# Decoder layer on one core: routed rows computed seven tiles early, their products no longer woven into the dense ones

## What is computed

```python
logits = xn @ router_w
topv, topi = jax.lax.top_k(jax.nn.softmax(logits, axis=-1), K)          # K = 2
...
for e in range(E):                                                      # E = 8
    out = out + comb[:, e:e + 1] * _swiglu(xn, gate_up_w[e], down_w[e]) # gate clipped to +-10
out = out + _swiglu(xn, shared_gate_up_w, shared_down_w)
x = _layernorm(x + out.reshape(b, s, d))
```

## Time and profile before

| what | value |
|---|---|
| median of 3 runs (lowest, highest) | 1808.25 us (1808.15, 1811.41) |
| the profiled execution itself | 1811.44 us |
| its span in the profile | 1809.7 us, mean granted TensorE clock 0.987 |
| PE busy | 1730.8 us, 96% of the span |
| DVE, ACT, POOL busy | 1485.6, 1105.6, 265.6 us |
| experts (PE's first to last matmul) | 1665.4 to 1801.6 us |

### The profile page before, as it was taken

How to read it: one execution, slowest core, us unless ns; L and a number is a source line. 1 busy time by engine, 2 the same in 40 slices (tenths; PEclk the granted TensorE clock), 3 DMA queues, 4 the chain that set the end, 5 groups by cost and what they waited for, 6 DMA issues and landing times.

```text
span 1809.7 us, 31511 instructions
## 1 busy us (share of the span) xinstructions
PE 1730.8 (96%) x9280; PEld 867.8 (48%) x9280; DVE 1485.6 (82%) x2398; ACT 1105.6 (61%) x1355; POOL 265.6 (15%) x344
## 2 busy tenths in 40 slices
PE   6977999999999999999999999999999999998896
PEld 4854444444444444444444444444444444444674
DVE  7868988888888888888878797979787888775777
ACT  4554666666666666666666666666666666665554
POOL 4746992000000000000000000000000000001443
PEclk8989999999999999999999999999999999999999
DMA  5001210000000000000000000000000000001000
GB/s 166 2 1 35 69 41 1 0 0 0 0 0 0 0 0 0 0 0 0 0 0 0 0 0 0 0 0 0 0 0 0 0 0 1 0 2 33 2 2 13
DMA packets 17753, 16.68 MB, mean 9 GB/s; under 512 B 6047, under 2 KB 15907, under 8 KB 17318
## 3 DMA queue, kind: packets, MB, share of 16 engines
q1 hardware_dynamic: 17446, 15.48, 2.8%
q0 software_dynamic: 256, 0.53, 0.1%
HBM read 13.95 MB, written 2.06 MB: 9 GB/s over the span
## 4 chain that ended last, share of the span: by engine, by line
PE 88%; DVE 6%; ACT 3%; issue 3%; POOL 0%; DVEq 0%; DMA 0%; SPq 0%; POOLq 0%; ACTq 0%
PE PS L1732 87%; ACT p_arena L931 1%; DVE mxs L1583 1%; DVE mxs L1319 1%; ACT p_arena L924 1%; DVE z_arena L1616 0%; DVE w_arena L1100 0%; DVE w_arena L1274 0%; ACT z_arena L767 0%; ACT p_arena L921 0%; DVE acc L1621 0%; POOL w_arena L587 0%; DVE m_arena L1280 0%; DVE z_arena L1607 0%; PE PS L1741 0%
## 5 line engine op out<-in xcount | busy, mean ns | idle before, releaser
L921 ACT ACTIVATE p_arena<-PS 128x1024 f16<-128x1024 f32 (+1 forms) x480 | 484.8, 1010 | 531.1 <-PE PS L1732 530.9
L1732 PE MATMUL PS<-a_arena,z_arena 128*128 (+1 forms) x2832 | 746.3, 380 | 4.4 <-DVE a_arena L1338 4.1
L1732 PE MATMUL PS<-p_arena,z_arena 128*128 128x512 f16 x2800 | 740.4, 379 | 1.4 <-ACT p_arena L931 0.3
L1319 DVE TENSOR_REDUCE mxs<-PS 128x512 f32 (+1 forms) x900 | 582.5, 668 | 91.0 <-PE PS L1732 87.7
L1351 DVE TENSOR_TENSOR p_arena<-p_arena 128x1024 f16<-128x1024 f32 (+1 forms) x480 | 574.8, 1198 | 98.0 <-ACT p_arena L924 90.8
L924 ACT ACTIVATE p_arena<-PS 128x1024 f32<-128x1024 f32 (+1 forms) x480 | 481.6, 1003 | 0.0
L1732 PEld LDWEIGHTS PS<-a_arena,z_arena 128*128 (+1 forms) x2832 | 274.8, 98 | 331.8 <-DVE a_arena L1338 4.4
L1732 PEld LDWEIGHTS PS<-p_arena,z_arena 128*128 128x128 f16 (+1 forms) x2800 | 269.2, 98 | 311.9 <-ACT p_arena L931 8.8
L1732 PE MATMUL PS<-z_arena,a_arena 128*128 (+3 forms) x1024 | 353.8, 361 | 10.5 <-DVE mxs L1319 8.2
L699 POOL IOTA a_arena<- 128x512 f16 x1 | 0.6, 558 | 1289.8 <-DVE acc L1362 1289.8
L1732 PEld LDWEIGHTS PS<-z_arena,a_arena 128*128 (+1 forms) x1024 | 97.8, 98 | 144.0 <-DVE mxs L1319 26.5
(11 more groups left out here) (324 smaller groups left out, 1014.8 us busy)
## 6 DMA issues: line engine op xcount, KB each, us to landing
w_arena<-in_L_ffn_gate_up_w SPq DMA_DIRECT2D x8, 512.0 KB, 3.6
p_arena<-in_ctx SPq DMA_DIRECT2D x2, 1600.0 KB, 9.0
w_arena<-in_L_ffn_down_w SPq DMA_DIRECT2D x8, 256.0 KB, 4.0
a_arena<-in_L_xattn_Wkv SPq DMA_DIRECT2D x1, 1024.0 KB, 5.8
xg_dram<-VO SPq DMA_DIRECT2D x1, 975.0 KB, 8.8
w_arena<-in_x SPq DMA_DIRECT2D x1, 512.0 KB, 4.3
a_arena<-in_L_xattn_Wo SPq DMA_DIRECT2D x1, 512.0 KB, 6.8
w_arena<-in_L_xattn_Wq SPq DMA_DIRECT2D x1, 512.0 KB
```

The costliest lines, as they stand in the source:

```text
L921: s.activation(Phi[:, r % 3, 0:w], ps, ACT.Exp, scale=1 / SSC).then_inc(hi_ready, 1)
L1319: v.tensor_reduce(mxs[:, i, bass.ds(kb, 1)], PS[:, 6 + par, 0:w], AX.X, ALU.max).then_inc(mx_read, 1)
L1732: return t.matmul(o, l, r, start=start, stop=stop)
```

## The change

- The woven form is gone: every unit writes its whole gate, then small work part 0, then its whole up product, then part 1.
- Seven slots instead of four stand between shared 0 and shared 1, and the other eight follow one behind each of the first eight dense units (experts 0 and 1) instead of two per expert up to expert 5. `COMB_END` is unit 30 instead of 43.
- The norm of the second half starts behind clip 0, two pieces in each of units 0 to 3; its transpose moves from unit 2 to 5, its router from 5 to 10, its exponential from 9 to 14. The end of the first half goes in ten pieces instead of five.
- In the last block the first half's transposes move from step 4 to 5, its router from 6 to 8, what follows by two steps each, and the transposes of its first slots from step 25 to behind the last step.

```diff
-AHEAD = 4
+AHEAD = 7
...
         for i in range(4):
             order.append(("dense", e, i))
-            if i % 2 == 0 and k < SLOTS:
+            if k < SLOTS:
                 order.append(("slots", k, 0))
...
         for t in ALL_TILES:
-            put(p + 3 + t // 2, t % 2, "shared", half, t)
-    put(2, 1, "turned", 1, 0)
-    put(5, 1, "routed", 1, 0)
+            put(p + 3 + t, 1, "shared", half, t)
+    put(5, 1, "turned", 1, 0)
+    put(10, 1, "routed", 1, 0)
```

ACT (`half_act(0, 0)` from step 6 to 7, `half_act(0, 1)` from step 9 to 11; in the units):

```diff
-                if u == 3:
+                if u == 6:
                     half_act(1, 0)
-                elif u == 9:
+                elif u == 14:
                     half_act(1, 1)
```

DVE, `half_in_block` (one shift of two steps from the routing on), `half_done` and `side_work`:

```diff
-                elif st == 5:
+                elif st == 6:
                     dve.wait_ge(ld_fv, N_FV)
                     dve.wait_ge(xfT_ps, 1)
                     turned(0, 6).then_inc(xfT_v, 1)
-                elif st == 7:
+                elif st == 9:
                     turned_low(0)
...
-                    for t in ALL_TILES:
+                if piece < 2:
+                    for t in (2 * piece, 2 * piece + 1):
                         last = v.tensor_tensor(acc[:, t, :], acc[:, t, :], PS[:, COMB, t * P:(t + 1) * P], ALU.add)
                     last.then_inc(comb_read, 1)
-                    dve.wait_ge(comb_read, 1)
-                    half_norm(0, 0, twice=False)
-                elif piece < 4:
-                    half_norm(0, 2 * piece - 1, twice=False)
-                    half_norm(0, 2 * piece, twice=False)
                 else:
-                    half_norm(0, 7, twice=False)
+                    if piece == 2:
+                        dve.wait_ge(comb_read, 2)
+                    half_norm(0, piece - 2, twice=False)
...
-                if u == 0:
-                    half_norm(1, 6)
-                    half_norm(1, 7)
-                elif u == 4:
+                if u < 4:
+                    if u == 0:
+                        dve.wait_ge(o_acc, 2 * NBLK)
+                    half_norm(1, 2 * u)
+                    half_norm(1, 2 * u + 1)
+                elif u == 7:
                     turned_low(1)
-                elif u in (5, 6):
-                    half_norm(1, u + 3)
-                if 6 <= u < 9:
-                    route(1, u - 6)
-                elif 11 <= u < 15:
-                    route(1, u - 8)
-                elif 0 <= u - COMB_END < 5:
+                elif u in (8, 9):
+                    half_norm(1, u)
+                elif 11 <= u < 14:
+                    route(1, u - 11)
+                elif 15 <= u < 19:
+                    route(1, u - 12)
+                elif 0 <= u - COMB_END < 10:
                     half_done(u - COMB_END)

-            for piece in range(6):
-                if piece == 0:
-                    dve.wait_ge(o_acc, 2 * NBLK)
-                half_norm(1, piece)
```

PE:

```diff
-                    if end and st == 4:
+                    if end and st == 5:
                         pe.wait_ge(o_acc, 2 * (NBLK - 2))
                         half_turned(0, 6).then_inc(xfT_ps, 1)
-                    if end and st == 6:
-                        half_routed(0, 7).then_inc(rt_ps, 1)
...
-            gate_done = False
             for u in range(NUNITS):
-                if not gate_done:
-                    plain(u, 0)
-                small_work_pe(u, 0)
-                gate_done = WEAVE and u + 1 < NUNITS and (ORDER[u][0] == "slots") != (ORDER[u + 1][0] == "slots")
-                if gate_done:
-                    woven(u)
-                else:
-                    plain(u, 1)
-                small_work_pe(u, 1)
+                for o in range(2):
+                    plain(u, o)
+                    small_work_pe(u, o)
```

More of the change, by code:

```diff
@@ L67 @@
 SLOTS = 15
-WEAVE = True
 ROW = 2 * D + 4
-AHEAD = 4
+AHEAD = 7
 def unit_order():
@@ L944, in block_act @@
                     weights(j, st)
-                    if st == 6 and end:
-                        half_act(0, 0)
                     if st == 1 and not first:
@@ L952, in block_act @@
                             weights(j, Turn(i, k))
-                            if (i, k) == (0, 2):
+                            if (i, k) == (0, 0):
+                                half_act(0, 0)
+                            elif (i, k) == (0, 4):
                                 half_act(0, 1)
@@ L1519, in half_in_block @@
                     route(0, 0)
-                elif st == 8:
+                elif st == 10:
                     route(0, 1)
                     route(0, 2)
-                elif st == 9:
+                elif st == 11:
                     hot(0)
-                elif st == 10:
+                elif st == 12:
                     route(0, 3)
-                elif st == 11:
+                elif st == 13:
                     hot(1)
-                elif st == 12:
+                elif st == 14:
                     hot(2)
-                elif st in (13, 14):
-                    rows_split(st - 13)
-                    if st == 14:
+                elif st in (15, 16):
+                    rows_split(st - 15)
+                    if st == 16:
                         hot(3)
-                elif 15 <= st < 18:
-                    hot(st - 11)
-                elif st == TAIL:
+                elif 17 <= st < 20:
+                    hot(st - 13)
+                elif st == NS - 1:
                     for f in range(2):
@@ L2150, in block_pe @@
                         values_low(NS * j + st - 2, LOOP0 + k - 2, i)
-                        if st == 10:
+                        if st == 8:
+                            half_routed(0, 7).then_inc(rt_ps, 1)
+                        elif st == 12:
                             pe.wait_ge(cnt_ready, 1)
@@ L2160, in block_pe @@
                             half_rows(xfhi[0], 7).then_inc(hot_ps, 1)
-                        elif st == 13:
+                        elif st == 15:
                             pe.wait_ge(hot_read, 1)
@@ L2189, in block_pe @@
                         max_to_row(b)
-                    if st == TAIL and end:
+                    if st == TAIL + 2 and end:
                         pe.wait_ge(hot_read, 3)
-                        for f in range(2):
-                            slots_turned(f, 6 + f).then_inc(xt_ps, 1)
-                    if st == TAIL + 2 and end:
-                        pe.wait_ge(xt_sb, 2)
                     if st == TAIL + 3 and end:
@@ L2279, in _ @@
             block_pe(NBLK - 1, maxes=False, nxt=False, end=True)
+            pe.wait_ge(o_acc, 2 * (NBLK - 1))
+            for f in range(2):
+                slots_turned(f, 6 + f).then_inc(xt_ps, 1)
             for r in (NS - 2, NS - 1):
@@ L2282, in _ @@
                 values_low(NS * (NBLK - 1) + r, r)
-            pe.wait_ge(o_acc, 2 * (NBLK - 1))
+            pe.wait_ge(xt_sb, 2)
             project(NBLK - 1, 0)
@@ L2348, in plain @@
                         dense_product(u, o, n, bank)
-            def woven(u):
-                ready(u + 1)
-                up, gate = free_bank(u, 1), free_bank(u + 1, 0)
-                if ORDER[u][0] == "slots":
-                    for blk in range(4):
-                        if blk < 3:
-                            dense_product(u + 1, 0, blk, gate)
-                        slots_products(u, 1, blk, up)
-                else:
-                    for blk in range(4):
-                        if blk < 3:
-                            dense_product(u, 1, blk, up)
-                        slots_products(u + 1, 0, blk, gate)
             def down(hid_hi, hid_lo, his, los, o):
@@ L2445, in _ @@
             pe.wait_ge(f_hid, LAST_UNIT)
-            pe.wait_ge(comb_read, 1)
+            pe.wait_ge(comb_read, 2)
             for t_ in ALL_TILES:
```

## The result

The changed kernel takes **1805.77 us** (median of 7 runs, 1801.83 to 1806.68) against 1809.02 for the kernel before on the same chip (7 runs, 1808.15 to 1812.12): ratio 0.9971, 95% interval 0.9958 to 0.9984, which is 5.3 us less (2.9 to 7.6 by the interval). The ratio goes with the means, which differ by 5.2 us; the medians differ by 3.3. The forecast was 5.2 less; its median of 1803.0 was missed by 2.8. The profiled execution took 1805.96 us, span 1803.9, against 1811.44 and 1809.7.

The account below looks back on a forecast made before the run. PE is busy 96% of the span, so only its idle stretches can give time: experts' loss 29.0 to 25.9 us (-3.1), last block -2.1, together -5.2, median 1808.25 to 1803.0 us; range 1794 to 1811.

Parts of the forecast that it names:

- Last block, -2.1: Attention's last block: PE's waits of 1.24 and 0.84 us both go, nothing is late next, 2.1 us less.
- Start of the experts, 9.1 lost: Head of the experts: DVE 3.2, address groups 4.0, turned second half 0.4, POOL 1.5; 9.1 us lost against 9.0 before.
- In units 4 to 7 three such groups each (gate, y, up) have nothing wide between them: 12 by 0.33 = 4.0 us: Head: twelve narrow groups with computed addresses, not hidden behind wide matmuls, each lose 0.33 us, 4.0 in all.
- Nothing won: Head of the experts: the wait and low clock are exchanged for DVE and addresses, 9.1 us lost against 9.0 before.
- POOL on the norm's pieces, 0.5 a unit: Head: the norm's small operations run beside POOL and are held, 0.5 us for each of three units, 1.5 us.
- Eight pairs, 4.0: Eight pairs of a dense unit and a slot: addresses only partly hidden, 0.5 us lost per pair, 4.0 us.
- routing, 3.5: Routing's exponential: two ACT table loads of 1.28 us delay silu and y behind them, 3.5 us lost, from 2.1 before.
- Dense chain, 4.6: 24 dense units: chain from gate to next up is too long in six units, 0.77 us each, 4.6 us lost.
- End of the first half, 3.5: Units 30 to 39: DVE becomes the bound by its pieces; 3.5 us added with POOL's share, 8 by 0.44.
- B: Rival, 17%: nothing won, DVE bounds wherever it has side work; head 1.5 and pieces 2.7 us more, 1807.
- C: Rival, 17%: slower, address groups bind throughout (pairs 4.0 more), low clock stays for the head (5.0 more), 1812.0.
- A: Rival, 15%: more is won, the sequencer gets its lead and POOL rarely meets a piece; -16 us, 1792.

Follow-up runs that it names:

- experiment 5: The changed kernel with each slot tile's down product (y) half a unit later: 1806.61 us against 1812.31 for the kernel before, ratio 0.9973.
- experiment 8: Kernel before plus block moves, a slot tile behind each of the first eleven dense units, ten small end pieces; four tiles ahead, woven: 1800.37 us, ratio 0.9936.
- experiment 7: Kernel before with only the second half's norm moved behind the first two clips: 1811.08 us against 1812.31, ratio 0.9994.
- experiment 12: The kernel of experiment 9 with the second half's norm behind the first two clips: 1799.07 us, ratio 0.9938 to the kernel before.
- experiment 2: Kernel before without weaving, shared expert's pieces one to a unit, some dense experts' pieces half a unit earlier: 1819.24 us, ratio 1.0049.
- experiment 10: The kernel of experiment 8 without weaving, shared expert's pieces one to a unit: 1807.88 us, ratio 0.9986 to the kernel before.
- experiment 3: The changed kernel with weaving put back, in the changed order: 1805.38 us, ratio 0.996 to the kernel before.
- Experiment 6: The changed kernel with the second half's routing weights from the already loaded Silu table: 1803.4 us, ratio 0.9952 to the kernel before.
- experiment 11: The kernel of experiment 8 with the end of the first half in five large pieces: 1804.62 us, ratio 0.997 to the kernel before.
- experiment 4: The changed kernel with the end of the first half in five large pieces as before: 1809.65 us, ratio 0.9998 to the kernel before.
- the ninth: The kernel of experiment 8 with the second half's routing weights from the Silu table: 1799.32 us against 1808.96 for the kernel before, ratio 0.9936.
- experiment 1: Kernel before with the moves in the last block alone: 1808.6 us against 1810.99, ratio 0.9985.

## Why the prediction was right, point by point

The sum was right (-5.2 forecast, -5.3 measured) and so was the length of the experts (133 forecast, 133.45). Its terms were not all, and that they added up is luck.

**Last block, -2.1: right.** No wait ahead of transposes or router, nothing late next; alone it gave 2.4.

**Start of the experts, 9.1 lost: too little, and a step was missing.** By the prediction's own pitches, 1662.26 to 1690.97 (start of the second shared unit) holds 6 wide and 252 narrow matmuls and four transposes, 1.3 + 14.1 + 0.5 = 15.9 of 28.7 us: 12.8 lost. What was foreseen came: the second clip behind the norm's first pieces (at 1665.38, earlier than the 1667 to 1669 of the forecast) and the third at 1668.61, slot groups of 1.10 to 1.25 us, waits of 1.07 and 0.76 for DVE. The failed step is "In units 4 to 7 three such groups each (gate, y, up) have nothing wide between them: 12 by 0.33 = 4.0 us": it counts TensorE's groups only, and not the three small banks, whose emptying hangs on the next unit's clip. They gave 2 x 1.40 us and a stretch at 1.2 GHz; experiment 5 removed these waits and got others. "Nothing won" was too friendly: experiment 8 against the change says that seven tiles ahead, the norm behind the clips and the unweaving together lose 3.6 us, and experiments 7 and 12 that the norm's place is worth 0 to 0.5 of it in the other direction. Which part makes the ring's waits of 1.4 us in the head is settled in part: experiments 2 and 10 have them with four tiles ahead, experiment 3 with the weave (its units there are slots behind slots, with nothing to weave). All kernels that have them have the shared expert's pieces one to a unit, and a woven kernel with four tiles ahead and that placement was not run.

**POOL on the norm's pieces, 0.5 a unit: right in the head.** It hit two, 0.9 and 0.8 us over their 0.17. DVE's longer one, and the next beside it:

```profile
1667.26 0.17 DVE L1390 TENSOR_TENSOR rs<-rs,wt_arena 128x8 f32<-128x8 f32 x1
1667.46 1.12 DVE L1392 SCALAR_TENSOR_TENSOR wt_arena<-rs,wt_arena 128x8 f32<-128x8 f32 x1
```

POOL's subtraction ran from 1667.40 for 1.16 us. The Trainium skill, page "SBUF — State Buffer", section "Who interferes with whom", says that the later of two such operations waits for the earlier; the trace agrees for each that met POOL, but few of them do.

**Eight pairs, 4.0, and routing, 3.5: near.** The stretch from 1690.97 to 1737.7 holds 54 wide and 453 narrow matmuls and the router, 37.6 of 46.7 us: 9.1 lost against 7.5. Experiment 6 gives 3.1 for the routing, the low clock behind its wait included, and 1.6 without it (last section). Experiment 3 gives 2.8 for weaving the pairs, 0.35 each instead of 0.5, and experiment 10 2.3. The groups of twelve without addresses last 0.83 us as before, so the pitch is still 0.056. The Trainium skill's 62 ns of sequencer time for each matmul with hardware decode off ("TensorE: Matmul & The Clock Gate", "Wait — 56ns, not 53.3ns?") is not in these traces.

**Dense chain, 4.6: too much.** "Six such" by 0.77 were four by 0.6 to 0.7, and one of 0.16.

**End of the first half, 3.5: wrong.** The step is "In these units DVE becomes the bound by its pieces (2.4 to 2.6 a unit against PE's mean of 2.0)". From the thirty-second to the forty-first clip a unit took (1772.10 - 1752.71) / 9 = 2.15 us, and PE waited for DVE 0.8 us in all. It also charged the small pieces with POOL's share, of which 0.2 us came. What it did not see is that the large pieces had that share: the earlier trace rows is one of three operations that GpSimd held in the kernel before, 2.7 us in all. The size of the pieces is the most valuable part of the change, 4.2 to 4.8 us (experiments 11 and 4), and ten of them need the order, since before only six units were left behind the last slot tile.

So the experts lost 133.45 - 107 = 26.4 us against 25.9, but as 12.8, 9.1 and, for the rest, 4.5, where the forecast had 9.1, 7.5 and 9.3. (Counted by its own 144 wide and 385 narrow matmuls the rest lost 5.4: the "about 2" for transposes and router is some 0.8 too much.) The errors, 3.7 and 1.6 too low and 4.8 too high, cancelled. The experiments add up to the same: 2.4 for the block, 2.5 for the order alone, 4.2 for the small pieces, less the 3.6 of experiment 8 against the change, 5.5 us. Of the rivals, B had 1.5 more in the head, and 3.7 more came, but 2.8 of it as waits of the ring, in which DVE stands too and is not the bound that B has; its 2.7 in the pieces did not come; C's low clock came for about 3 us, twice, not for the head; A did not come, but the parts without the change's head (experiments 8 and 9, ratio 0.9936) gain 11.6 of its 16 us.

**The version that beats both** is the ninth: 1799.32 against 1808.96 us in its job, ratio 0.9936 where the change has 0.9971, and experts 6.0 us shorter than the change's. The eighth has the same ratio without touching the routing's arithmetic; the twelfth is no different.

## What to carry to other kernels

When a change has several parts, price each with and without the others: here small pieces were worth 4 us and the new head cost 3.6, and the sum hid both; unweaving cost nothing in one order and 7.6 us in another. Ask of side work not only how long it is but what it runs into: three of the five large pieces met GpSimd and lost 0.9 us each, of the ten small ones one did, for 0.2. Count what circles between two engines (a few banks that one fills and the other empties behind its next main step) beside each engine's work: two engines can both stand idle with neither full, and a product moved half a unit only moves the wait. And a table load on a shared ScalarE queue costs what stands behind it; look for a function in the table that is loaded.

## What the hardware showed that was not expected

The same wait did not always bring the low clock. In the changed kernel and in experiment 4, PE waited 2.8 us for the same product, busy 1.62 and 1.61 us in the 4 us up to it. Behind it the clock was 0.50 and 0.64 in the one (rows under experiment 6) and 1.00 in the other:

```profile
1717.50:1719.50 2.00, 2.00 (x36) 1.90 (x34) 0.57 (x3) 0.71 (x2) 1.20 (x2) 1.00 0.00 0
1719.50:1721.50 2.00, 2.00 (x31) 1.65 (x29) 2.00 (x5) 0.63 (x1) 0.00 (x0) 1.00 0.03 8
```

The unit took 4.56 us in the first and 3.19 in the second, so the low clock alone cost 1.4. Experiment 6 has neither the wait nor the low clock: from the sixteenth to the twenty-second clip it is 3.1 us shorter than the changed kernel and 1.6 shorter than experiment 4, so one and the same wait is worth 3.1 or 1.6 us. The kernel before and experiment 1 show it again: both wait 2.13 us for DVE L1496, behind it the clock is 1.00 in the one and 0.63, then 0.51 in the other, and the second unit behind the wait takes 2.21 against 3.24 us. A single trace can't tell which is usual, and differences of less than 1 us between the experts' lengths of two kernels say little.
